# The additive attention mask of a decoder layer, opened in PSUM by matmuls of 64 x 64 blocks in place of 32 x 32 blocks

## What is computed

```python
x = x + rbf_attention(layernorm(x), Wq, bq, Wk, bk, Wv, bv, Wo, bo)
x = x + cross_attention(ctx_1024, ctx_1024, layernorm(x), mask, ...)
x = x + moe(layernorm(x), Wg, W1, b1, W2, b2)

def cross_attention(values, keys, query, mask, ...):      # 16 heads of 16
    v, k, q = (split_heads(t @ W + b) for t, W, b in ...)
    energy = einsum('nqhd,nkhd->nhqk', q, k)
    energy = where(mask == 0, finfo(float32).min, energy)
    attn = softmax(energy / sqrt(16), axis=-1)
    out = einsum('nhqk,nkhd->nqhd', attn, v)
    return out @ Wo + bo
```

## Time and profile before

| | us |
|---|---|
| runs | 637.98, 638.79, 631.1 |
| median | 637.98 |
| the profiled execution: its time | 637.98 |
| the profiled execution: its span, first to last instruction | 636.2 |
| PE busy in the span | 565.9 (89%) |
| DVE busy | 358.8 (56%) |
| ACT busy | 330.0 (52%) |
| POOL busy | 221.0 (35%) |
| mean granted TensorE clock | 0.939 |

### The profile page before, as it was taken

One profiled execution on the slowest core, in us unless ns is written; L12 is line 12 of the kernel. 1 busy time (PEld: TensorE's weight loads), 2 busy tenths in 40 slices (PEclk: granted clock), 3 DMA queues, 4 the chain that ended last, 5 costly groups with the idle time before them and its releaser, 6 DMA issues.

```text
span 636.2 us, 16617 instructions
## 1 busy us (share of the span) xinstructions
PE 565.9 (89%) x5619; PEld 490.3 (77%) x5620; DVE 358.8 (56%) x856; ACT 330.0 (52%) x723; POOL 221.0 (35%) x289
## 2 busy tenths in 40 slices
PE   3867989999999999865877899999999999999992
PEld 2755767777777777543444799999999999999991
DVE  3547776869696877647564877565233332323321
ACT  3532357665656474522352774555656556565560
POOL 6323121223232321000014514633555554555542
PEclk9988899999999999968576799999999999999997
DMA  9575543444526261721156945666676676766732
GB/s 233 137 102 114 68 68 53 77 78 67 87 58 96 52 103 27 110 69 35 41 179 229 325 150 166 176 183 212 179 206 208 175 227 175 212 200 183 227 88 25
DMA packets 56172, 85.90 MB, mean 135 GB/s; under 512 B 6704, under 2 KB 44880, under 8 KB 56112
## 3 DMA queue, kind: packets, MB, share of 16 engines
q1 hardware_dynamic: 46368, 73.59, 45.2%
q0 software_dynamic: 7872, 10.33, 8.5%
q10 hardware_dynamic: 1872, 1.18, 0.7%
HBM read 62.44 MB, written 9.31 MB: 113 GB/s over the span
## 4 chain that ended last, share of the span: by engine, by line
PE 73%; DVE 8%; ACT 4%; DMA 4%; issue 4%; SPq 3%; POOL 1%; ACTq 1%; POOLq 0%; DVEq 0%
PE pair L2218 21%; PE bank L2258 16%; PE bank L1105 14%; PE bank L1485 4%; PE pair L1351 4%; PE pair L1450 4%; SPq L1424 3%; DVE row_max L1393 2%; PE pair L1381 2%; DMA q_stack<-max_lo 2%; PE bank L1074 2%; PE bank L2182 1%; PE bank L1577 1%; ACT exp_ring L1467 1%; DMA experts_w<-L_ffn_W 1%
## 5 line engine op out<-in xcount | busy, mean ns | idle before, releaser
L2218 PE MATMUL pair<-slots_t,w_now 128*128 128x128 f32 x1248 | 147.4, 277 | 0.0
L2218 PEld LDWEIGHTS pair<-slots_t,w_now 128*128 128x128 f32 x1248 | 144.1, 194 | 0.0
L2228 ACT ACTIVATE hid<-pair,b_tile 128x128 f32<-128x128 f32 x312 | 88.7, 367 | 54.5 <-PE pair L2218 54.5
L2238 DVE TENSOR_TENSOR hid_lo<-hid,hid_hi 128x1024 fp32r<-128x1024 f32 x39 | 47.8, 1225 | 107.5 <-ACT hid_hi L2235 107.5
L2171 POOL DMA_INDIRECT out<-y,scatter_now x39 | 63.8, 1636 | 112.8 <-DMA out<-y,scatter_now 76.7
L1467 ACT ACTIVATE exp_ring<-pair 128x1024 f32<-128x1024 f32 x64 | 65.7, 1028 | 56.1 <-PE pair L1450 56.1
L1393 DVE TENSOR_REDUCE row_max<-pair 128x4 f32<-128x1024 f32 x64 | 78.2, 1222 | 27.3 <-PE pair L1381 27.3
L2258 PE MATMUL bank<-experts_w,hid_hi 128*128 x624 | 82.7, 285 | 0.0
L2258 PEld LDWEIGHTS bank<-experts_w,hid_hi 128*128 128x128 f32 x624 | 75.8, 188 | 0.0
L2235 ACT ACTIVATE hid_hi<-hid 128x512 fp32r<-128x512 f32 x78 | 49.3, 632 | 4.7
L2156 POOL DMA_INDIRECT slots_in<-xn_rows,gather_now x39 | 41.0, 1050 | 25.8 <-POOL gather_now L2153 15.4
(11 more groups left out here) (283 smaller groups left out, 1011.7 us busy)
## 6 DMA issues: line engine op xcount, KB each, us to landing
w_now<-L_ffn_W SPq DMA_DIRECT2D x39, 1024.0 KB, 5.0
experts_w<-L_ffn_W SPq DMA_DIRECT2D x8, 1024.0 KB, 6.2
k_stack<-ck_hi SPq DMA_DIRECT2D x32, 128.0 KB, 3.9
q_stack<-cq_hi SPq DMA_DIRECT2D x32, 128.0 KB, 4.3
ctx_in<-ctx SPq DMA_DIRECT2D x8, 256.0 KB, 2.8
k_stack<-ck_lo SPq DMA_DIRECT2D x16, 128.0 KB, 5.3
q_stack<-cq_lo SPq DMA_DIRECT2D x16, 128.0 KB, 5.2
out<-x SPq DMA_DIRECT2D x7, 256.0 KB, 4.9
```

Source lines behind the costliest of these rows:

```text
L2218: mm = eng.matmul(banks[half][:, f * P:(f + 1) * P], core.w1_now[b.p][:, c, start:start + P], core.slots_t[b.p][:, c, :], start=c == 0, st ...
L2228: act = eng.activation(core.hid[:, g, :], banks[half][:, f * P:(f + 1) * P], ACT.Relu, bias=core.b1_tile[b.p][:, g:g + 1])
L2238: core.m["hid_lo"].at(eng.tensor_tensor(core.hid_lo[b.p][:, :, :], core.hid[:, :, :], core.hid_hi[b.p][:, :, :].bitcast(F32), ALU.subtract))
```

## The change

`mask_product` uses the array in blocks of 64 x 64: each area is opened by four weight loads and four matmuls of 512 columns, two with the mask in place (shift 0) into bank 0 and two with the halves swapped into bank 1. Both `scores_open` and `exps_open` use the same four blocks, with masks of their own. There are two turned copies in place of three (one of `mask_q`, one of `mask_k`), made by four transfers of 64 partitions in place of six; the count for which TensorE waits follows. `mask_q` gets room of its own. The four masks take as much room as before. The waits and the order of the calls stay as they are.

```diff
-BLOCK = 32
-BLOCKS = P // BLOCK
...
+    core.mask_q = sb("mask_q", [KT, S], BF16)
     core.mask_k = sb("mask_k", [KT, S], BF16)
-    turned = [sb(f"mask_turned{i}", [KT, S], BF16) for i in range(1, BLOCKS)]
-    core.masks_k, core.masks_q = ((0, core.mask_k), (1, turned[0])), ((2, turned[1]), (3, turned[2]))
+    core.mask_q_turned = sb("mask_q_turned", [KT, S], BF16)
+    core.mask_k_turned = sb("mask_k_turned", [KT, S], BF16)
     core.max_hi = sb("max_hi", [S], F32R)
     core.max_lo = sb("max_lo", [S], F32R)
     core.one_rows = core.max_hi[0:1, :]
-    at = core.cursor
-    core.mask_q = sb("mask_q", [KT, S], BF16)
-    core.cursor = at
...
     e.wait_ge(E["masks_ready"], 1)
-    for shift, mask, turned in ((1, core.mask_k, core.masks_k[1][1]), (2, core.mask_q, core.masks_q[0][1]),
-                                (3, core.mask_q, core.masks_q[1][1])):
-        for first, count in ((0, BLOCKS - shift), (BLOCKS - shift, shift)):
-            here = slice(first * BLOCK, (first + count) * BLOCK)
-            start = (first + shift) % BLOCKS * BLOCK
-            loads(core, e, turned[here, :, :], mask[start:start + count * BLOCK, :, :], E["masks_turned"])
+    for mask, turned in ((core.mask_q, core.mask_q_turned), (core.mask_k, core.mask_k_turned)):
+        for r in range(2):
+            here, there = (slice(x * HALF, (x + 1) * HALF) for x in (r, 1 - r))
+            loads(core, e, turned[here, :, :], mask[there, :, :], E["masks_turned"])
...
-        eng.wait_ge(core.E["masks_turned"], 16 * 6)
+        eng.wait_ge(core.E["masks_turned"], 16 * 4)
...
-def mask_product(core, eng, pair, masks):
-
-    for c, (shift, mask) in enumerate(masks):
-        for r in range(BLOCKS):
-            rows, to = (slice(x * BLOCK, (x + 1) * BLOCK) for x in (r, (r + shift) % BLOCKS))
-            eng.matmul(pair[to, c * 512:(c + 1) * 512], core.ident_bf[rows, rows], mask[rows, :, :],
+def mask_product(core, eng, pair, mask, turned):
+
+    for c, part in enumerate((mask, turned)):
+        for r in range(2):
+            left = slice(r * HALF, (r + 1) * HALF)
+            to = left if c == 0 else slice((1 - r) * HALF, (2 - r) * HALF)
+            eng.matmul(pair[to, c * 512:(c + 1) * 512], core.ident_bf[left, left], part[left, :, :],
                        start=True, stop=False, skip_group_check=True)
...
-    mask_product(core, eng, scores_pair(core, b, i), core.masks_q)
+    mask_product(core, eng, scores_pair(core, b, i), core.mask_q, core.mask_q_turned)
...
-    mask_product(core, eng, exps_pair(core, b, i), core.masks_k)
+    mask_product(core, eng, exps_pair(core, b, i), core.mask_k, core.mask_k_turned)
```

## The result

The changed kernel takes 641.1 us (median of 20 runs, 638.93 to 643.15), the kernel before 637.67 us (20 runs, 631.1 to 639.75). The ratio is 1.0069 with a 95% interval of 1.0046 to 1.0094: 4.4 us slower, between 2.9 and 6.0. The medians alone lie 3.4 us apart, the means 4.4, since the runs of either kernel scatter by several us. The forecast was +4.0 us, 642.0. The profiled execution has a span of 642.9 us against 636.2, which is 2.3 us more than the ratio says.

What follows compares the result with a forecast made beforehand. The prediction took PE, busy 89% of the span, to bound the kernel: +5.2 us in the attention quads less 1.2 us in the set-up gives +4.0 us on 637.98, so 642.0 us, range 633 to 650.

Steps and rivals of the forecast that it cites:

- Second round: Attention openings: scores masks wait for blocks the exps masks use, starting 0.23 us after the first exps mask, formerly 0.05.
- A quad without a wait: Attention quad whose two areas both open without waiting: +0.18 us at full clock; 22 such quads pay, 3.96 us.
- The upper bound with weights loaded late: Second round of masks: loading weights into blocks in use adds up to 0.10 to 0.11 us.
- Rival 1: Openings: second-round weights come late, scores masks start at 0.33 us, +4.2 us more, so 646 us; chance 0.14.
- Change of shape: Between masks and products: the shape change costs 0.09 us, nothing saved, products 0.31 us after the last mask.
- rival 2: Masks to products: cheaper change of shape, 636.5 us, or 630.5 with both savings; chance 0.13, 0.04 of it both.
- Which quads pay: Attention iterations 2 to 8: of 29 quads without a wait 22 cost 0.18 us, 7 nothing; all quads together +5.2.
- absorbed quad 4: Quad 4, iterations 2 to 7: 0.19 us of slack before the row maxima on DVE covers the 0.18 loss.
- settled iteration: Attention iteration at full clock: from 32.80 to about 33.6 us, four quads at 0.18 plus 0.08 less 0.02.
- move with PE: Attention quads: most waits of PE start from PE itself, so they move with it and hide nothing.
- Set-up: Set-up: two ACT transfers fewer; first projection moves from 13.36 to 12.15 us, held by PE's transposes: -1.2 us.
- The sum: Whole kernel: +5.2 us on PE less 1.2 us in the set-up gives +4.0 us, 642.0 us.

Runs made afterwards that it cites:

- e1: Changed kernel with 32 x 32 blocks, the scores area using the same eight blocks as the exps area, four set-up transfers: 640.87 us, ratio 1.0062 to the kernel before.
- e5: Kernel before with one scores mask for all shifts and two set-up transfers; in quad 4 alone scores use the exps blocks: 636.07 us, ratio 0.9987.
- e0_after: The changed kernel again, unaltered, timed and profiled a second time against the kernel before: 641.55 us, ratio 1.0079.
- e6: Kernel before with one scores mask for all shifts and two set-up transfers; in quads 1, 2, 6, 7 scores use the exps blocks: 637.47 us, ratio 0.9993.
- e2: Changed kernel with its four set-up transfers cut into six, nothing else: 642.49 us, ratio 1.0107 to the kernel before.

## Why the prediction was right, step by step

**Second round.** Forecast 0.22 us after the first, measured 0.24 (0.23 with 32 x 32 blocks in e1). A quad without a wait cost 0.19 in place of 0.18. The upper bound with weights loaded late, 0.33, didn't happen: of that 0.11 only 0.02 was there, and the weights were in at 148.92, 0.10 before the second round. Rival 1 would have given 0.33. The Trainium skill ("TensorE: Matmul & The Clock Gate", Part 3) has the rule that weight loads overlap matmuls in flight only in another row group; the two PEld rows above, in the same row groups as the exps masks, don't bear it out.

**Change of shape.** The products come 0.31 us behind the last mask, as before. Nothing was saved, so rival 2 is out. (Its two sums should read 636.6 and 630.6; nothing hangs on it.)

**Which quads pay.** The absorbed quad 4 was right and is shown by e5. A settled iteration was forecast at 33.6 us and took 33.8. The excess is small pieces of one sign: 0.02 more on quad 0, 0.01 on each of four quads, 0.02 in quad 4, whose loss just exceeds the slack, and 0.01 to 0.04 behind quads 3, 6 and 7. Over iterations 2 to 8 the profile of the changed kernel has 7.3 us more than that of before and e0_after 7.1, where +5.2 was forecast. Of the excess of about 2, 0.7 is in the four settled iterations. The rest is in iteration 7 (0.9) and 8 (0.4) of the one profile and in iteration 8 (1.2) of the other, where the granted clock changes, so I don't put it down to the blocks; no run separates the two. For quad 2 the reasoning was incomplete: I had it paid because waits "move with PE". e6 shows that the wait behind it doesn't; in the changed kernel quad 2 is paid since the next quad's wait is spent on the blocks. The count of paid quads came out right by luck in this place.

**Set-up.** Forecast -1.2 us, with the first projection at 12.15; it came at 11.97, and by the first mask the gain was 1.9 (2.3 in e0_after). The step that was mis-sized is what is late next. The prediction had the transposes hold the projection back to 12.15; it started 0.78 us after the first of them instead of 0.93, so all of the 1.39 us by which `attnWqh` moved came through. What came on top came behind the first projection. Timeline of PE after, key and query projections:

```profile
13.85 1.05 PE L1099 MATMUL bank<-tr_lo,attnWkh 128*128 128x256 f32 x4
...
15.75 0.62 PE L1099 MATMUL bank<-tr_lo,attnWqh 128*128 128x256 f32 x4
```

The same four matmuls take 1.05 us and then 0.62. The spacing shortens at about 15.0 us, in the middle of the projections. In the profile of the kernel before all of them ran at the longer spacing, up to 18.65 us. I read this as the 1.2 and the 2.4 GHz level, from the durations alone: the mean granted clock is 1.00 from 10 to 31 us in both profiles and doesn't show it. Between 31 and 44 us part of the gain went back: the mean granted clock there is 0.74 after, and 0.87 in the like stretch before (33 to 46 us).

**The sum.** The two misses have opposite signs: 2 us too little cost for the iterations, 1 us too little gain for the set-up. The profiles that the sum was meant for lie 6.7 us apart, or 3.5 with e0_after. So the size, +4.0 against a measured +4.4, is in part luck; the mechanism is not, since settled iterations repeat it quad by quad.

**What stays open** is the rest of the 6.7 us between the two profiles. In the profile after TensorE fell to 1.2 GHz for a short while at the end of iteration 7 (mean granted clock 0.72 from 270 to 276 us, 1.00 in the like stretch before, 265.8 to 271.8). e0_after, the same program, didn't have it there: its iteration 7 took 30.4 us, not 31.3. I take this for the scatter of single executions; no run was made to test it.

## What to carry to other kernels

Before areas of PSUM are opened with small matmuls, count the blocks of the array that the whole burst wants, over all areas: 16 different blocks pass in the time of one matmul, while larger matmuls, with half the instructions, need a second round as soon as two areas want the same block. When a delay lands in front of a wait, ask what that wait and the next one are already used for, since a slack covers one delay and not two. Transfers issued by a compute engine in the set-up cost it about 0.67 us each, so a queue whose engine computes nothing should have them, though here the times don't show a gain.

## What I had not expected of the hardware

- The weight load of a second matmul in a block in use is almost free: it is done while the first one streams, and the second round starts 0.24 us after the first, where 512 columns alone need 0.22, and 0.43 at 1.2 GHz.
- Where the start of dense work moved, the pace of stretches far behind it changed too: with the first projection 1.4 us earlier the projections gained some and the stretch from 31 to 44 us lost some. From 31 to 38 us the mean granted clock is 0.89 before and 0.88 in e2, the two profiles whose first projection starts at 13.4 us, and 0.55 to 0.82 in the nine others, where it starts at 11.30 to 12.74. Why it falls there no run shows.
- Runs of one and the same kernel lie up to 8.7 us apart (the kernel before, 631.1 to 639.75), twice the effect measured here. So one profile of each kernel can't settle such a change, while the length of a settled iteration at the full clock repeats to 0.1 us.
